# Local attention on one Trainium2 core: where a slot applies the layer norm, takes the maxima and turns queries and keys

## The reference, cut to what matters

```python
for i in range(DEPTH):                      # DEPTH = 6
    x = attn_layer(shift_tokens(x), Wqkv[i], q_scale[i], k_scale[i], Wo[i]) + x
    x = ffn_layer(shift_tokens(x), ln_g[i], ln_b[i], W1[i], b1[i], W2[i], b2[i]) + x

# attn_layer: 16 heads of 64, window 32 (each query sees its own window and the one before)
q = l2norm(q) * qs;  k = l2norm(k) * ksc
q = q * cos * scale + rotate_half(q) * sin * scale        # k likewise with 1 / scale
sim = where(mask, -max, einsum(q, k) * 8);  out = softmax(sim) @ v;  return out @ Wo
# ffn_layer
xn = (x - mu) / sqrt(var + 1e-05) * g + bln
a, gate = split(xn @ W1 + b1, 2);  return a * gelu(gate) @ W2 + b2
```

## Time and profile before

| | us |
|---|---|
| median of 3 runs | 6022.95 (6012.32 to 6030.93) |
| the profiled execution | 6025.09 |
| span in its profile | 6023.3 |

### The profile page before, as it was taken

How to read it: one execution, slowest core, us unless ns; L and a number is a source line. 1 busy time by engine, 2 the same in 40 slices (tenths; PEclk the granted TensorE clock), 3 DMA queues, 4 the chain that set the end, 5 groups by cost and what they waited for, 6 DMA issues and landing times. The chain is left out here.

```text
span 6023.3 us, 112187 instructions
## 1 busy us (share of the span) xinstructions
PE 5290.3 (88%) x34984; PEld 3858.1 (64%) x34984; DVE 4948.4 (82%) x8818; ACT 4123.4 (68%) x12293; POOL 3433.0 (57%) x2277
## 2 busy tenths in 40 slices
PE   7999899999999999999999999999999997576666
PEld 6999666666666666666666666666666665333333
DVE  4666688889888898888888898888888885778877
ACT  3555477777777777777777777777777775555443
POOL 1222366666666666666666666666666662434444
PEclk9999899999999999999999999999999998788787
DMA  1000000000000000000000000000000000000000
GB/s 20 4 3 3 23 1 0 0 0 10 10 0 0 0 12 8 0 0 5 14 1 0 0 6 14 1 0 0 9 5 0 0 0 4 1 2 2 3 3 4
DMA packets 35423, 25.54 MB, mean 4 GB/s; under 512 B 11316, under 2 KB 29303, under 8 KB 35191
## 3 DMA queue, kind: packets, MB, share of 16 engines
q1 hardware_dynamic: 26302, 22.22, 1.2%
q10 hardware_dynamic: 8888, 0.45, 0.1%
HBM read 20.57 MB, written 2.10 MB: 4 GB/s over the span
## 5 line engine op out<-in xcount | busy, mean ns | idle before, releaser
L1145 POOL TENSOR_TENSOR b_w<-b_w,b_vt 128x512 f32<-128x512 f32 x768 | 980.8, 1277 | 1412.7 <-DVE b_vt L1054 778.9
L1149 POOL TENSOR_TENSOR b_rn<-b_ssm,all_neg_half 128x16 f32<-128x16 f32 x384 | 1126.8, 2934 | 32.0
L971 ACT ACTIVATE b_PT<-ps 128x512 f32<-128x512 f32 x768 | 461.2, 601 | 458.3 <-PE ps L826 457.6
L953 ACT ACTIVATE b_Pr<-ps,b_nm 128x128 f32<-128x128 f32 x1536 | 564.9, 368 | 287.5 <-DVE b_nm L1086 285.0
L1086 DVE TENSOR_REDUCE b_nm<-ps 128x4 f32<-128x640 f32 x768 | 630.8, 821 | 125.2 <-PE ps L806 113.5
L872 PE MATMUL ps<-b_Whi,b_xlo 128*128 128x512 f32 x1152 | 596.3, 518 | 91.2 <-DVE b_vt L1054 78.1
L955 ACT ACTIVATE b_Pr<-ps,b_nm 128x160 f32<-128x160 f32 x1536 | 611.2, 398 | 0.0
L1052 DVE TENSOR_TENSOR b_w<-ps,until_b_rotab 128x512 f32<-128x512 f32 x768 | 529.3, 689 | 26.4 <-ACT b_sq L986 6.1
L986 ACT ACTIVATE b_sq<-ps 128x512 f32<-128x512 f32 x768 | 468.0, 609 | 81.4 <-PE ps L874 80.9
L1054 DVE TENSOR_TENSOR b_vt<-ps,until_b_rotab 128x512 f32<-128x512 f32 x768 | 523.2, 681 | 0.0
L1056 DVE TENSOR_REDUCE b_ss<-b_sq 128x8 f32<-128x512 f32 x768 | 519.7, 677 | 0.0
(11 more groups left out here) (256 smaller groups left out, 13935.0 us busy)
## 6 DMA issues: line engine op xcount, KB each, us to landing
b_Wraw<-in_L_ffn_Wqkv SPq DMA_DIRECT2D x36, 256.0 KB, 2.9
b_Wo<-in_L_ffn_Wo SPq DMA_DIRECT2D x6, 512.0 KB, 4.1
a_xtok<-in_L_attn_hidden_states SPq DMA_DIRECT2D x16, 128.0 KB, 2.1
out<-c_xout SPq DMA_DIRECT2D x16, 128.0 KB, 1.8
b_W<-in_L_ffn_W SPq DMA_DIRECT2D x6, 341.0 KB, 2.9
setup_wmod<-in_L_wmod SPq DMA_DIRECT2D x2, 384.0 KB
b_W<-in_L_ffn_W SPq DMA_DIRECT2D x6, 128.0 KB
setup_rot<-in_rot SPq DMA_DIRECT2D x1, 256.0 KB
```

Of the source, the lines that this page charges most:

```text
L953: nc.scalar.activation(s.Pr[:, p % 2, j, 0:P], ps[:, S_BANK[j], WIN:KEYS], ACT.Exp, bias=s.nm[:, h, 0:1], accum_out=s.ssum[:, h, 0:1])
L1145: nc.gpsimd.tensor_tensor(rows, rows, s.vt[:, i % 4], ALU.add).then_inc(s.pool_add, 1)
L1149: nc.gpsimd.tensor_tensor(s.rn[:, j], s.ssm[:, j], g.neg_half[:, 0:HB], ALU.pow).then_inc(s.pool_r, 1)
```

## The change

It makes four edits in `phase_b`: the DVE's `normalise` of the third block moves from slot 13 to slot 14; DVE's block for the row maxima moves ahead of the block for the layer norm's statistics in the slot loop; on PE, the turnings of `TRANSPOSE_SLOT` move ahead of the piece, and those of `LATE_SLOT` to just behind the piece, ahead of the tail's products and the values.

```diff
-DVE_NORM_SLOT = {13: 2}
+DVE_NORM_SLOT = {14: 2}
...
                             give_spare(("w2", 0), last)
+                    if step.front is not None and slot in TRANSPOSE_SLOT:
+                        transpose_qk(f, TRANSPOSE_SLOT[slot])
                     if step.front is not None and slot in PIECE_SLOT:
...
                         nc.tensor.matmul(ps[:, F_BANK[k % 2]], s.xhi[:, pf, rows], s.Whi[:, cols], start=False, stop=True).then_inc(s.proj_done, 1)
+                    if step.attn and slot in LATE_SLOT:
+                        transpose_qk(n, LATE_SLOT[slot])
                     if step.tail is not None:
...
                         values(item, p, pa if slot >= PAIR_PV else 1 - pa)
-                    if step.front is not None and slot in TRANSPOSE_SLOT:
-                        transpose_qk(f, TRANSPOSE_SLOT[slot])
-                    if step.attn and slot in LATE_SLOT:
-                        transpose_qk(n, LATE_SLOT[slot])
...
                         nc.vector.tensor_scalar_mul(s.lnp[:], ...).then_inc(s.lnp_ready, 1)
+                    if step.attn and slot % 2 == 0:
+                        ...  # the maxima: wait for s_done, TENSOR_REDUCE to s.nm, max_done
                     if step.tail is not None and slot == STATS_SLOT:
                         ...  # copy to s.xtok and statistics
-                    if step.attn and slot % 2 == 0:
-                        ...
```

More of the change, by code:

```diff
@@ L1076, in body @@
                         nc.vector.tensor_scalar_mul(s.lnp[:], g.lparam[:, bass.ds(lt, 1), 0:2].rearrange("p a k -> p (a k)"), 1.0).then_inc(s.lnp_ready, 1)
+                    if step.attn and slot % 2 == 0:
+                        p = slot // 2
+                        dve.wait_ge(s.s_done, HPAIRS * n + p + 1)
+                        nc.vector.tensor_reduce(s.nm[:, 2 * p:2 * p + 2], ps[:, S_BANK[0]:S_BANK[1] + 1, 0:TT * KEYS].rearrange("p j (t k) -> p j t k", t=TT),
+                                                AX.X, ALU.max, negate=True).then_inc(s.max_done, 1)
                     if step.tail is not None and slot == STATS_SLOT:
```

## The result

| | before | after |
|---|---|---|
| median of the runs, us | 6019.05 (6012.32 to 6030.93, 4 runs) | 5794.77 (5792.16 to 5796.74, 4 runs) |
| profiled execution, us | 6025.09 | 5792.16 |
| its span, us | 6023.3 | 5790.3 |
| mean granted clock of PE over the span | 0.953 | 0.962 |
| busy: PE, DVE, POOL, us | 5290, 4948, 3433 | 5208, 4944, 3339 |

Forecast were 5815 us in a range of 5775 to 5955.

A forecast was written before the change was run, and what follows sets the result against it. PE was taken as the bound, starving in slots 12 to 14. 93 steps x 1.7 = 158 us plus 50 for the clock gave 208 off 6025: 5817, against the median 5815 us; range 5775 to 5955.

The forecast's parts named there:

- Product from slot 13 to 14: DVE's normalise of the third block, moved, frees POOL's gate and the applies, so xn and scores come earlier: 1.7 us per step.
- the 2028.9: Slots 13 to 14 on POOL: predicted end of the gate product at its own 1.80 us, in place of 2029.74.
- `lnp` waits for the add: Slot 14 on DVE: the small copy ahead of the maxima waits for POOL's add, so the maxima start at 2030.15.
- the alternative: Slot 14 on DVE: the small copy doesn't wait for POOL's add; then 1.9 us per step are gained.
- Maxima, front turnings, late turnings: DVE's maxima block and PE's turnings changing places with neighbouring blocks: 0 us forecast for each.
- the bound of 0.7 us a step: PE's swapped turnings: the most a reader of a delayed piece, value or turned block could lose.
- PE waiting at L799 for L955: Sign of a right forecast: PE's scores (L799) wait for the exponentials, meant ahead of the next step's scores.
- Clock: PE's 1.2 GHz stretches, blamed on the pause before xn: between 0 and 65 us come back, 50 taken.
- The rival with the clock unchanged: PE's remaining pauses in slots 12 to 14 still bring the 1.2 GHz level: 5865 us, chance 0.15.
- The power holds the port: POOL's power in slot 14 holds back the moved normalise, so nothing is gained: about 6023 us, chance 0.05.
- the slower rival: POOL's power holds the moved normalise and the gate isn't shortened: 0.75 us per step lost, 6093 us, chance 0.07.
- the long gate: POOL's gate is long for another reason, so only xn moves: 5930 to 5953 us, chance 0.13.

The follow-up runs named there:

- norm_only: The kernel before with only the third block's normalise moved from slot 13 to 14: 5794.78 us, ratio 0.9613.
- no_gate: The kernel before with POOL's gate product cut to 16 columns, so W2 reads ungated numbers: 5823.95 us, ratio 0.9666.
- no_third: The changed kernel with the third block's layer norm product cut to 16 columns: 5792.68 us.
- lnp_early: The changed kernel with the copy `lnp` moved nine slots earlier, behind the residual of slot 5: 5778.99 us, ratio 0.9588.
- norm_front: The changed kernel with the turnings of `LATE_SLOT` put back behind the values: 5794.06 us, ratio 0.9612.
- fill7: The kernel before with 7 idle 128 by 128 products on PE ahead of its wait for the layer norm's applies: 5969.21 us, ratio 0.9904.
- turns_only: The changed kernel with the third block's normalise back in slot 13, leaving the moved turnings and maxima: 6086.9 us, ratio 1.009.

## Why the prediction was right

*Product from slot 13 to 14: 1.7 us a step forecast, 1.90 measured.* The chain went as written: gate at its own length, applies in the two gaps beside it, xn behind the last transpose, W2 and END earlier, the product in END's idle time under the power. norm_only shows that it is this edit, no_gate that the gate's hold is what makes the applies late, no_third that the new place is free. The 0.2 us too little are all in when the maxima start; counted from slot 14's scores, they start 0.22 us earlier than worked out. The working let the first apply push the gate by 0.1 us; the gate was not pushed and ended 0.15 us earlier than the 2028.9. It let the maxima start at the add's end; they start 0.05 us ahead of it. Behind them the links came as written: 0.85 us to the exponentials, 1.55 through them, 0.06 to the scores. PE's own work is just as late there, and that is why lnp_early, with its maxima 1.1 us earlier, gained only 0.17.

*`lnp` waits for the add.* It does, 1.26 us for a copy of 0.16 to 0.23. But the alternative was mis-sized: with the wait gone the forecast gave 1.9 in place of 1.7, and the gain per step in fact went from 1.90 to 2.07.

*Maxima, front turnings, late turnings: 0 forecast.* 0 measured beside the moved product (norm_only against after, norm_front). Without it the turnings cost 57 us, outside the 0 and within what the bound of 0.7 us a step allowed, but by a way that the prediction did not name: not a late reader, but the clock. Made by themselves, they would have been forecast wrong. And the sign "PE waiting at L799 for L955" came true at another place than the chain meant: at slot 14, from the front turnings.

*Clock: 50 forecast, 48 measured.* The reason given was that the drop came behind the 1.85 us pause. fill7 supports it: the pause filled, the shorter ones left, and all but two of the 28 slow stretches gone. The number is luck. The prediction left 8 us of its 73 to the five layer changes, and took 50 of the other 65 as coming back. The layer changes in fact take 22.5 us in the changed kernel, where the clock is never low, and 25 in fill7. So only some 48 us were the clock's, and all of them came back. The two errors cancel. The rival with the clock unchanged (5865 us) is out.

*The power holds the port.* Out: the product took 1.225 us at the median of 176, half of them inside a power, its own length. The Trainium skill's "SBUF — State Buffer", section "SBUF: two separate sides", names no exception for such an instruction; for the adds and the gate the trace agrees with it, for the power it doesn't (the power reads SBUF, and a DVE product with two SBUF inputs ran inside it at full speed). With this out, the slower rival falls too, and the long gate is out by the gate's 1.81 us at the median.

The sum: 93 x 1.7 + 50 = 208 forecast, 233 in the spans: 175 in place of 158 from the step, 48 in place of 50 from the clock, and 10 in the steps around those 92 and phase C, which had no term.

Open: why turns_only is given the lower clock more often, 58 stretches against 28. Its pauses in slots 12 to 14 are four (3.43 us a step in sum) where before's are three (3.09 us). Whether their number, their sum or their distance counts was not tried.

## What to carry to other kernels

Where VectorE and GpSimd both work in SBUF, compare each small instruction's duration with its minimum, and look whose end it falls on. Here a product of 1.23 us cost 1.9 us a step where it stood: it held back GpSimd's gate, and the gate then held the layer norm on VectorE. The cheapest place for it was idle time beside the power, which doesn't hold VectorE. Pauses of PE as long as the 1.85 us here can have a second price, in its clock; filling it with idle products of known length measures that price before anything is moved. Test an edit that "costs nothing" without its companions as well: here one that was free in the changed kernel cost 57 us in the old one.

## What the runs showed of the hardware that was not expected

- A copy of 128 by 2 numbers on DVE took 1.26 us with POOL's whole add beside it, 0.47 with the last of the add, and 0.16 to 0.23 with neither: this small copy pays what is left of POOL's add, whatever its own size. A DVE sum over 512 columns of SBUF (L1056) doesn't: it took 0.67 to 0.68 us inside an add and outside.
- POOL's power of 2.93 us held no DVE product with two inputs in SBUF: the moved one took 1.225 us inside it, as at slot 0 outside it, and the spread of the reciprocals (L1107) 0.69 us inside and outside.
- POOL's recorded time includes its wait: a product of 16 columns took 1.20 us behind a DVE product, and the gate 2.79 or 1.80 for the same work.
- A waiting DVE instruction gets in between two POOL instructions that stand back to back: both applies did, in each step.
- 7 idle products of PE in a pause of 1.85 us made the kernel 56 us faster (ratio 0.9904), and 14 made it 61 us slower.
